# Cross attention and soft mixture of experts on one core: turned probabilities kept in five places, value products over groups of 2, 3 and 2 tiles, second layer inside the attention loop

## The reference, cut to what matters

```python
x = x + attn(layernorm(x), ctx)        # x (8, 56, 128), ctx (8, 1500, 128), 16 heads of 64
# attn: q = x @ Wq, k = ctx @ Wk, v = ctx @ Wv; softmax(q k^T / 8) v @ Wo
h = layernorm(x)
logits = h @ phi_w.T + phi_b           # (tokens, 64, 32)
D = softmax(logits, slots of an expert)     # over 32
C = softmax(logits, experts)                # over 64
X = clip(sum over all tokens of D * h)      # (64, 32, 128)
X = tanh(layernorm(X))
Y = X @ expert_w + expert_b
x = x + sum over slots of C * Y
```

## Time and profile before

| | |
|---|---|
| median of 3 runs | 473.62 us |
| profiled execution | 472.34 us |
| its span, first to last instruction | 470.5 us |
| PE busy | 438.3 us, 93% |
| PE weight loads busy | 381.7 us, 81% |
| DVE busy | 343.8 us, 73% |
| ACT busy | 256.0 us, 54% |
| POOL busy | 125.2 us, 27% |

### The profile page before, as it was taken

The page is one execution under the profiler, slowest core; times in us unless marked ns, Lnnn a source line. Parts: engine busy times, 40 slices in busy tenths (PEclk is TensorE's granted clock), DMA queues, the critical chain, the costliest instruction groups (busy, mean ns, idle before and its releaser), DMA issues.

```text
span 470.5 us, 7401 instructions
## 1 busy us (share of the span) xinstructions
PE 438.3 (93%) x2776; PEld 381.7 (81%) x2776; DVE 343.8 (73%) x596; ACT 256.0 (54%) x439; POOL 125.2 (27%) x64
## 2 busy tenths in 40 slices
PE   2899899999999999999999998999999998888577
PEld 1788788898889888988998887888887886677467
DVE  2367777877686777777767786776589999999850
ACT  1366565565565655656555566655657664245442
POOL 0508000313050005031300223033030351997520
PEclk9999999999999999999999999999999999999799
DMA  7110100010001000100100013000000000970000
GB/s 218 45 67 1 67 1 0 1 65 1 1 3 64 1 1 24 43 0 0 60 6 0 0 65 89 3 2 0 1 0 2 0 1 5 296 146 1 1 1 21
DMA packets 8495, 15.38 MB, mean 33 GB/s; under 512 B 290, under 2 KB 4274, under 8 KB 8468
## 3 DMA queue, kind: packets, MB, share of 16 engines
q1 hardware_dynamic: 6996, 12.91, 9.4%
q10 hardware_dynamic: 1472, 2.10, 1.5%
HBM read 14.78 MB, written 0.23 MB: 32 GB/s over the span
## 4 chain that ended last, share of the span: by engine, by line
PE 71%; DVE 15%; DMA 4%; ACT 4%; POOL 4%; issue 1%; SPq 0%; POOLq 0%
PE turned L589 14%; PE scores L577 7%; PE scores L579 7%; PE scores L578 7%; PE acc L607 7%; PE acc L609 7%; PE acc L608 7%; PE misc L521 3%; DMA ctx_raw<-in_ctx_dram 3%; DVE bankmax L1305 3%; DVE pT_l L1314 2%; PE misc L623 2%; PE misc L515 2%; ACT prob L1041 2%; DVE cmax L1357 2%; DVE csum L1374 2%
## 5 line engine op out<-in xcount | busy, mean ns | idle before, releaser
L1314 DVE TENSOR_TENSOR pT_l<-turned,pT_h 125x512 fp32r<-125x512 f32 x168 | 112.1, 687 | 65.7 <-ACT pT_h L1034 65.3
L1034 ACT CAST pT_h<-turned 125x512 fp32r<-125x512 f32 x168 | 95.2, 591 | 112.8 <-PE turned L589 112.7
L1305 DVE TENSOR_REDUCE bankmax<-scores 128x1 f32<-128x500 f32 x168 | 110.4, 674 | 20.9 <-PE scores L579 20.6
L589 PEld LDWEIGHTS turned<-ident,prob 128*125 128x125 f32 x672 | 88.4, 187 | 14.6 <-DVE pT_l L1314 8.5
L589 PE MATMUL turned<-ident,prob 128*125 128x128 f32 x672 | 94.4, 276 | 2.3 <-DVE pT_l L1314 2.2
L1041 ACT ACTIVATE prob<-scores,negmax 128x1500 f32<-128x1500 f32 x56 | 85.0, 1519 | 9.9 <-DVE negmax L1308 9.8
L607 PE MATMUL acc<-pT_h,ctx_nh 125*128 125x384 f32 (+1 forms) x192 | 78.3, 408 | 0.0
L386 POOL TENSOR_TENSOR ctx_nh<-ctx_raw,zero 125x1536 fp32r<-125x1536 f32 x8 | 22.0, 2745 | 184.3 <-PE acc L609 169.3
L609 PE MATMUL acc<-pT_h,ctx_nl 125*128 125x384 f32 (+1 forms) x192 | 70.1, 365 | 0.0
L608 PE MATMUL acc<-pT_l,ctx_nh 125*128 125x384 f32 (+1 forms) x192 | 69.9, 364 | 0.0
L577 PE MATMUL scores<-ctx_th,qk_h 128*128 128x500 f32 x168 | 69.3, 412 | 0.6 <-DVE qk_l L1298 0.3
(11 more groups left out here) (172 smaller groups left out, 560.9 us busy)
## 6 DMA issues: line engine op xcount, KB each, us to landing
ctx_raw<-in_ctx_dram SPq DMA_DIRECT2D x7, 750.0 KB
eb<-in_L_ffn_expert_b_dram SPq DMA_DIRECT2D x4, 256.0 KB, 8.0
ctx_raw<-in_ctx_dram SPq DMA_DIRECT2D x3, 250.0 KB
wq_sb<-in_L_xattn_Wq_dram ACTq DMA_DIRECT2D x1, 512.0 KB, 4.9
wk_sb<-in_L_xattn_Wk_dram ACTq DMA_DIRECT2D x1, 512.0 KB, 8.2
wv_sb<-in_L_xattn_Wv_dram ACTq DMA_DIRECT2D x1, 512.0 KB, 9.1
wo_sb<-in_L_xattn_Wo_dram ACTq DMA_DIRECT2D x1, 512.0 KB, 14.9
x_sb<-in_x_dram SPq DMA_DIRECT2D x1, 224.0 KB, 5.3
```

Of the source, the lines that this page charges most:

```text
L589: last = tr(turned[0:CK, m, 128 * c:128 * c + 128], prob[u][:, CK * j:CK * j + CK], ident[:, :])
L1034: nc.scalar.copy(pT_h[0:CK, t, CPB * k:CPB * k + CPB, :], turned[0:CK, (KB * u + k) % 2, :].rearrange("p (c r) -> p c r", c=CPB)).then_inc ...
L1305: m = v.tensor_reduce(bankmax[:, u, k:k + 1], scores[:, k, 0:KW], AX.X, ALU.max)
L1314: v.tensor_tensor(pT_l[0:CK, t, dst, :], turned[0:CK, (KB * u + k) % 2, :].rearrange("p (c r) -> p c r", c=CPB), pT_h[0:CK, t, dst, :].bit ...
```

## The change

The value groups become tiles 0 and 1, 2 to 4, 5 and 6. The turned probabilities have NP = 5 places in place of 7, and a table, PLACES, says where a tile of an even or odd item lies. That frees 24 KB of each partition, in which logit0, disp0, logit1 and small statistics get buffers of their own. 6 chunks of a group stand in each of tiles 0, 1, 2 and 6, 4 in each of tiles 3 to 5; in item 7 all 12 of the second group stand in tile 6.

`spread_rden` moves from PE and ACT to SP: two DMAs for each group, rden to a row in DRAM, and that row back to rbc on all partitions, with the tiles of a group interleaved; only the very last group is spread by PE as before. `normalise` moves on DVE from the end of a tile to the place behind the tile's maxima.

The second layer of q = 0, 1 and 2 is placed in items 2 to 7: phi turned in item 2, logits of q = 0 in item 4, of q = 1 in item 6, of q = 2 in item 7, with their maxima and sums; `combine_shift` of q = 0 and 1 moves from DVE to POOL. The hardware loops are written out. At the end, PE turns the combine weights of q = 0, 1 and 2 ahead of the slots' turn, and the output goes in two parts.

```diff
-    GROUPS = ((0, 3), (3, 7))
+    GROUPS = ((0, 2), (2, 5), (5, 7))
+    NG = len(GROUPS)
+    NP = 5
+    PLACES = ((0, 1, 2, 3, 4, 0, 1), (3, 4, 0, 1, 2, 3, 4))
...
-        pT_h, pT_h_at = take("pT_h", [128, NT, NC, 128], F32R)
-        pT_l, pT_l_at = take("pT_l", [128, NT, NC, 128], F32R)
+        pT_h, pT_h_at = take("pT_h", [128, NP, NC, 128], F32R)
+        pT_l, pT_l_at = take("pT_l", [128, NP, NC, 128], F32R)
...
-        rbc, rbc_at = take("rbc", [128, 512])
+        rbc, rbc_at = take("rbc", [128, 384])
+        rden_row = nc.dram_tensor("rden_row", [NG, 128, 3], F32, kind="Internal").ap()
+        logit0, phi_at = take("logit0", [PT, SLOTS])
+        disp0, disp0_at = take("disp0", [PT, SLOTS])
+        logit1, _ = take("logit1", [PT, SLOTS])
+        _, stat0_at = take("stat0", [PT, 96])
+        _, stat1_at = take("stat1", [PT, 96])
...
+            def spread_rden(n, a, grp):
+                t0, t1 = GROUPS[grp]
+                w = t1 - t0
+                row = rden_row[grp].rearrange("r t -> (r t)")[0:128 * w]
+                sp.wait_ge(rden_dve, n)
+                sp.dma_start(row.rearrange("(r t) -> r t", t=w), rden[:, a * NT + t0:a * NT + t1]).then_inc(rden_out, 16)
+                sp.wait_ge(rden_out, 16 * n)
+                wait(sp, oT_dve, n - 1)
+                sp.dma_start(rbc[:, 0:128 * w], row.partition_broadcast(128)).then_inc(rbc_in, 16)
             load_ctx(1)
-            with sp.Fori(1, PAIRS) as i:
-                load_ctx(2 * i)
-                load_ctx(2 * i + 1)
-            sp.wait_ge(qk_pe, 4 * PAIRS)
-            sp.dma_start(phi_sb[:, :, :], phi_w.rearrange("(k p) d -> p k d", p=128)).then_inc(phi_in, 16)
             sp.wait_ge(bias_zero, 1)
             for p in (0, 32):
                 sp.dma_start(b_raw[p:p + BR, :], phi_b.rearrange("(c e) -> c e", c=BR)).then_inc(bias_in, 16)
-            sp.wait_ge(pv_pe, 2 * B)
-            sp.dma_start(ew[:, :, :], expert_w.rearrange("n d h -> d n h")).then_inc(ew_in, 16)
+            sp.dma_start(phi_sb[:, :, :], phi_w.rearrange("(k p) d -> p k d", p=128)).then_inc(phi_in, 16)
+            for b in range(B):
+                if b > 0:
+                    spread_rden(NG * b, (b + 1) % 2, 2)
+                spread_rden(NG * b + 1, b % 2, 0)
+                if b + 2 < B:
+                    load_ctx(b + 2)
+                spread_rden(NG * b + 2, b % 2, 1)
...
+            split_ctx(2, 0)
+            split_qk(1)
+            split_ctx(3, 1)
+            root(1, 0, 1)
+            split_ctx(4, 0)
+            split_qk(2)
+            split_ctx(5, 1)
             dispatch_shift(0)
+            combine_shift(0)
+            root(2, 1, 2)
+            pool.wait_ge(x2n_dve, 2)
             dispatch_scale(0)
             combine_scale(0)
+            split_ctx(6, 0)
+            split_qk(3)
+            split_ctx(7, 1)
             dispatch_shift(1)
+            combine_shift(1)
+            root(3, 2, 3)
+            pool.wait_ge(x2n_dve, 3)
             dispatch_scale(1)
+            combine_scale(1)
             dispatch_shift(2)
             combine_shift(2)
             dispatch_scale(2)
+            combine_scale(2)
+            root(4, 3, 4)
...
-            def context_product(b, a, grp, chunks, by_bank=False):
+            def context_product(b, grp, chunks, by_bank=False):
+                a = b % 2
                 t0, t1 = GROUPS[grp]
+                p0 = PLACES[a][t0]
+                p1 = p0 + t1 - t0
...
-                    wait(pe, oT_dve, b * 2 + grp)
+                    wait(pe, oT_dve, NG * b + grp)
...
+            def mid_step(b, t):
...
+                if b in (4, 6) and t == 0:
...
+                    logits(q, 0)
+                if b in (2, 4, 6) and t == 6:
+                    turn_y((b - 2) // 2, M1)
+                if b in (3, 5, 7) and t == 1:
+                    turn_x2n((b - 3) // 2, M1)
...
+            def share(b, t):
+                if t == 0:
+                    return (b - 1, 1, range(6, NC)) if b > 0 else None
+                if t <= 2:
+                    return (b - 1, 2, range(6 * t - 6, 6 * t)) if b > 0 else None
+                if t == 6:
+                    return (b, 1, range(6)) if b < B - 1 else (b, 1, range(NC))
+                if b == 0:
+                    return (b, 0, range(6 * t - 24, 6 * t - 18)) if t > 3 else None
+                return (b, 0, range(4 * t - 12, 4 * t - 8))
...
-                    if 1 <= t <= 3 and not first:
-                        share = (b - 1, 1 - a, 1, range(4 * t - 4, 4 * t))
-                    elif t >= 4 and last:
-                        share = (b, a, 0, range(4 * t - 16, 4 * t - 12))
-                    elif t >= 4:
-                        share = (b, a, 0, range(3 * t - 12, 3 * t - 9))
-                    elif t == 0 and not first:
-                        share = (b - 1, 1 - a, 0, range(9, NC))
...
+            def ffn_step(b, t):
+                if b in (2, 4, 6) and t == 6:
+                    residual((b - 2) // 2)
+                if b in (3, 5, 7) and t == 0:
+                    q = (b - 3) // 2
+                    layernorm_apply(q + 1, x_sb, x2n, q, q + 1, x2n_dve)
+                if b in (4, 6) and t == 3:
+                    dispatch_max((b - 4) // 2)
+                if b in (4, 6) and t == 4:
+                    combine_max((b - 4) // 2)
+                if (b, t) == (5, 0):
                     dispatch_sum(0)
+                if (b, t) == (5, 2):
                     combine_sum(0)
+                if (b, t) == (6, 6):
+                    dispatch_sum(1)
+                if (b, t) == (7, 2):
+                    combine_sum(1)
+                if (b, t) == (7, 4):
+                    dispatch_max(2)
+                if (b, t) == (7, 5):
+                    combine_max(2)
+                if (b, t) == (7, 6):
+                    dispatch_sum(2)
...
                     row_max(g, u)
-                    if not (first and t == 0):
+                    if t == 1 and not first:
+                        normalise(b - 1, 1)
+                    if t == 3 and not first:
+                        normalise(b - 1, 2)
+                    if t == 6:
+                        normalise(b, 0)
+                    if g > 0:
                         lo_probs(g - 1, 1 - u, (t - 1) % NT, 0)
-                    if a == 0 and t == 0 and not first:
-                        lo_qk(i, 3, 1)
-                    if a == 1 and t == 1 and not last:
-                        lo_qk(i + 1, 0, 0)
-                    if 3 <= t <= 5 and not last and not first:
-                        lo_ctx(b + 1, 1 - a, t - 3, (t - 2 + a) % 2)
-                    if a == 1 and 5 <= t <= 6 and not last:
-                        lo_qk(i + 1, t - 4, (t - 4) % 2)
-                    if ending:
-                        early(a, t)
-                    if not (first and t == 0):
+                    if t == 0 and not first:
+                        invert(b - 1, 2)
+                    if t == 2:
+                        invert(b, 0)
+                    if t == 5:
+                        invert(b, 1)
+                    if 2 <= t <= 4 and b < B - 1 and not first:
+                        lo_ctx(b + 1, 1 - a, t - 2, 0)
+                    if a == 1 and 3 <= t <= 6 and b < B - 1:
+                        lo_qk(i + 1, t - 3, 1)
+                    ffn_step(b, t)
...
-                    if t == 0 and not first:
-                        normalise(b * 2 - 1, 1 - a, 0)
-                        invert(b * NT, 1 - a, 1)
-                    if t == 3 and not first:
-                        normalise(b * 2, 1 - a, 1)
-                    if t == 5:
-                        invert(b * NT + 3, a, 0)
...
-            invert(G, 1, 1)
-            normalise(2 * B - 1, 1, 0)
+            invert(B - 1, 2)
+            normalise(B - 1, 1)
             lo_probs(G - 1, 1, NT - 1, 0)
             lo_probs(G - 1, 1, NT - 1, 1)
             lo_probs(G - 1, 1, NT - 1, 2)
-            combine_max(1)
-            combine_shift(1)
-            dispatch_sum(1)
-            normalise(2 * B, 1, 1)
-            dispatch_max(2)
-            combine_sum(1)
-            residual(3, LAST, NQ, M0)
-            layernorm_apply(3, x_sb, x2n, LAST, NQ, x2n_dve)
-            combine_max(2)
+            combine_sum(2)
+            normalise(B - 1, 2)
+            residual(LAST)
+            layernorm_apply(NQ, x_sb, x2n, LAST, NQ, x2n_dve)
```

596 lines of the change are left out of this document (224 added, 372 removed).

## The result

The changed kernel takes 496.74 us (median of 4 runs, 493.56 to 500.76), the kernel before 474.10 beside it: ratio 1.0472, 95% interval 1.042 to 1.0523. The forecast was 487 us with a range of 475 to 498: the direction and the range hold, the middle is 9.7 us low. The median lies 1.3 us under the top of the range, and one of the four runs above it. The profiled execution took 493.56 us (span 491.8), 21.2 more than the one of before; that is the number to hold against the forecast's sum of +14.0.

The account below looks back on a forecast made before the run. PE, busy 93% of the span, was taken to bound the loop, a DVE, POOL and ACT chain the end; +22.5 and -8.5 gave +14.0 on 472.34 us, plus 1.3 for the median, rounded down to 487 us, range 475 to 498.

Parts of the forecast that it names:

- The new wait: Tiles 1, 3, 6: PE's next group's product waits for normalise behind negmax, 0.74 or 0.85 us each, 22 waits, +16.0.
- the rival in which it is hidden: Products at tiles 1, 3, 6: waits for normalise hidden, the 16.0 go, 487 becomes 471, faster; chance 0.09.
- The strided read: Normalise reads every second or third word of rbc: taken as 0, range keeps 6.6; rival with late rbc 0.12.
- DVE's passes: Items 4 to 7: ten DVE passes over logits, 33 us, make PE wait; +12.0, bounds 4 and 17.
- The old waits: Loop, third bank's turn waiting for the first's low part: of 8.5 us 1.5 kept, -7.0.
- Value products: Until the last value product: 256-column steps of 0.119 us make products dearer, 107.0 to 114.1, +7.1.
- the wait for phi: Item 6 in the loop: PE's wait for phi goes, -1.4.
- Spread: Loop: 54 of 56 PE turns of 1/den go to DMA, at 0.099 us each, -5.3.
- Logits piece: One more piece of second-layer logits moves from the end into the loop on PE, +1.1.
- From yt to the end: Last stretch, 32.2 us before: csum and scaling of group 2 go, one part less at the end, -3.9.
- the signs named for a wrong forecast: PE's product starting behind the turns without a gap, plain items under 44.4 us, or the end shrinking by over 13.
- those for a right one: 22 waits for oT, plain items 45 to 46, step 0.12, items 4 to 6 48 to 53, idle PE in item 7.

Follow-up runs that it names:

- normalise early: Changed kernel with DVE's normalise back at the end of the tile in which its group ends; 477.11 us, ratio 1.0067.
- alone: Changed kernel with DVE's loop passes over logits of q = 0, 1, 2 reading one column, normalise left as changed; 483.79 us, ratio 1.0184.
- both edits: Changed kernel with normalise at the end of the group's last tile and DVE's loop passes over logits cut to one column; 470.42 us, ratio 0.9875.
- the second profile: Changed kernel run again, unchanged; 497.62 us (6 runs), ratio 1.0513.
- the run with a warm PE: Changed kernel, normalise at the tile's end, plus unread identity products on PE, 9 before the projection and 8 before xt's first turn; 475.91 us, ratio 1.0037.

## Why the prediction was right, and where it was off

**Up to the last product: +22.5 forecast, +26.5 measured.**

- *The new wait*: 16.0 forecast, 16.6 by the edit that takes it away. Its place, its count (22 forecast, 21 in the list of waits) and its size (16.8 / 21 = 0.8) were right; the rival in which it is hidden is excluded. The strided read, taken as 0, is 0.8 of it, far from the 6.6 at the price of a stride of 32.
- *DVE's passes*: 12.0 forecast, 9.6 alone and 10.6 with normalise early. Items 4 to 6 were costed at 2.3, 2.5 and 2.7, measured 2.5, 2.2, 2.5; item 7 at 4.5, measured 3.4. The chain by hand, tile by tile, held within a quarter. (The ten passes it counts are eleven; their 33 us are right.)
- *The old waits, -7.0*: **this step failed.** It counted as time of PE. That row is of PEld, weight loads, which lie beside PE's work, and the earlier trace rows already said so: PE busy 44.38 of 44.38 us in the item. The row of PE itself, before:

```profile
PE turned L589 <- DVE pT_l L1314: 2.2, 4, 0.8
```

  Two of these four waits are in item 0 and two in the last tile of item 7; none is in a plain item. And the weight loads with both edits:

```profile
PEld turned L614 <- DVE pT_l L1239: 2.4, 6, 0.6
```

  So the waits of the weight loads went, 6.1 of 8.5 us, nearly as the prediction says, but PE's path got only the two waits of item 0 back, 1.8 us from start to start. In a plain item PE's turns take 8.4 us before and 8.3 to 8.5 with both edits. The 5.2 that did not come are more than the 4.0 missing; the other terms gave 1 back.
- *Value products*: +7.1 forecast. The table has 122.0 before, with 1.4 of the wait for phi and the 1.8 of item 0 in it, and 125.8 with both edits: +7.0 without these, and -1.4 for phi as forecast. In a plain item they take 16.2 us with both edits, 16.1 before, so the 0.4 per item was too much; the rest lies in items 0 and 7, where more products lie ahead of the last one than before. The step of 0.12 was right.
- *Spread*: -5.3 forecast, -5.4 where PE is full. *Logits piece*: +1.1, +1.1.

**The end: -8.5 forecast, -5.5 measured.**

- Last product to projection: -4.2 forecast, 11.2 to 7.2 measured.
- The projection ran at 1.2 GHz for most of its time, 5.42 us in place of 3.83, which was not foreseen; projection to x2n is +0.4 and not -0.6. To the first yt: -1.6, forecast -1.8.
- From yt to the end: -3.9 forecast, -0.3 measured. This is the second step that failed. The sum took out csum of group 2, but DVE had time for it: in the kernel before it stood behind the first yt, and the second yt still waited for PE.

```profile
445.27 0.69 DVE L1520 TENSOR_TENSOR yt<-acc,eb 128x512 f32<-128x512 f32 x1 [1.07 <-PE acc L950]
```

  And the sum took out the last part and forgot that the first one grew from 224 to 336 columns. The last of its four pieces, before:

```profile
456.71 1.78 PE L960 MATMUL scores<-combT,yt 128*128 128x224 f32 x8 [1.33 <-DVE yt L1520]
```

And after:

```profile
480.02 2.53 PE L922 MATMUL scores<-combT,yt 128*128 128x336 f32 x8 [2.23 <-DVE yt L1438]
```

  Three such pieces are 0.75 us more each, and the first, at half clock in both kernels, took 4.85 against 3.35. From yt to yt the rows give +1.0, +0.7 and 0.0 (the third piece lies beside DVE's csum of group 3, which stands there in both), and -2.1 from the last yt to the end. That this makes up the 3.6 was read off rows and not tried by a run; the run with a warm PE shows that the clock alone is worth 4.1 in the whole end.

The profiled execution is +21.2 against +14.0. The median lies 3.2 above it, not 1.3; item 7's half clock, which added 4.3 in the second profile, is the likely cause. So 497 us in place of 487 is 7 from the sum and 2 to 3 from that. The range held, but not for its own reasons alone: its upper end allows 6 for strided reads and 5 for a poor end, of which 0.8 and 3.0 came; the 5.2 us missing from the old waits were not in it, and that they found room is luck. Of the signs named for a wrong forecast none came; of those for a right one, the last product's start (415.97, forecast 410 to 413) and the length of the end (75.8, forecast 72) were missed, and the plain items (46.1, and 47.8 for item 2; forecast 45 to 46) lie a little above.

## What to carry to other kernels

A wait of weight loads is not by itself a wait of the matrix engine (here 6.1 us of them went, and PE's path got 1.8 of it back, where PE itself had stood): before a wait is booked as a gain, see whether the engine has a gap in that stretch at all. A consumer's result that frees the one accumulator belongs a whole phase ahead of the next user: moving 0.4 to 0.7 us of DVE's work, 22 times, from behind a tile's maxima to ahead of them was worth 16.6 us. In items 4 and 6 a pass cost what it exceeded the slack of its tile by: whole, the passes cost 5.0 us in these two, in pieces laid by the measured slack 0.2, in pieces laid without it 2.4 (the dsum of item 6 moved on to item 7 in the second case).

## What the runs showed that was not expected

- PE's clock fell to 0.50 behind gaps in which PE waited for DVE (tile 6 of item 7: 1.30 us busy of 3.40 ahead of it), and the penalty differs between executions of one kernel: item 7 up to the last product took 55.92 and 60.22 us. 17 products of the identity, 4.2 us on an idle PE, kept it at 1.00 in the profiled execution and made the end 4.1 us shorter.
- The start of the loop differs by up to 3 us between executions. The column of the granted clock shows 1.00 there, but PE's own rows say that the clock is the cause. Five of the setup's products, in an early execution (normalise early) and in a late one (nine warm products):

```profile
17.40 0.82 PE L562 MATMUL turned<-wkT,wqT 64*128 64x128 f32 x5
```

```profile
17.51 1.43 PE L562 MATMUL turned<-wkT,wqT 64*128 64x128 f32 x5
```

  Behind the first of the five, the distance from start to start is 0.11 us in one and 0.21 in the other, a ratio of nearly two like that of the two clock levels; the 16 products of the projection behind them (L546) take 2.01 and 3.75 us. In both executions PE steps at the slow rate from its first product on. In the early ones it changes to the fast rate at 17 to 18.5 us, in the late ones at 25 to 27.5, after the loop has begun. Why it changes at one time or the other stays open.
- A row of 256 or 384 single words written to DRAM lands in 8.2 to 8.7 us (median), in pieces of two or three words in 2.4 to 3.1.
